# An adaLN attention and mixture-of-experts block in fp32: a reordered seam before the first expert, split products in the prologue, and a reordered expert loop

## What is computed

```
mod = silu(c) @ wmod -> sa, ca, ga, sb, cb, gb        (4 x 512 each; ga, gb kept off zero)
h = layernorm(x) * (1 + ca) + sa
x = x + ga * attention(h)       16 segments of 128 tokens per batch: softmax(Q K^T * scale) V in each,
                                plus attention among the segments' first tokens, times Wo, biases
h = layernorm(x) * (1 + cb) + sb                       8192 tokens x 512
score = softmax(h @ Wg + bg)    16 experts; gate = max, idx = argmax
pos = rank of the token within its expert; keep = pos < 512
y = relu(h @ W1[idx] + b1[idx]) @ W2[idx] + b2[idx]    W1 512 x 2048, W2 2048 x 512 for each expert
x = x + gb * where(keep, y * gate, 0)
```

## Time and profile before

| | before |
|---|---|
| median of 3 runs | 1816.24 us (1816.03 to 1816.32) |
| the profiled execution | 1814.79 us |
| its span | 1813.2 us |
| PE busy | 1779.8 us (98%) |
| DVE busy | 1112.3 us (61%) |
| ACT busy | 893.4 us (49%) |
| POOL busy | 610.1 us (34%) |
| mean granted clock of TensorE | 0.995 of full |

### The profile page before, as it was taken

One profiled execution on the slowest core, in us unless ns is written; L12 is line 12 of the kernel. 1 busy time (PEld: TensorE's weight loads), 2 busy tenths in 40 slices (PEclk: granted clock), 3 DMA queues, 4 the chain that ended last, 5 costly groups with the idle time before them and its releaser, 6 DMA issues.

```text
span 1813.2 us, 27903 instructions
## 1 busy us (share of the span) xinstructions
PE 1779.8 (98%) x9135; PEld 1489.6 (82%) x9136; DVE 1112.3 (61%) x1964; ACT 893.4 (49%) x1317; POOL 610.1 (34%) x565
## 2 busy tenths in 40 slices
PE   9999999999999799999999999998998999999998
PEld 5788888888888488898888888888888888888886
DVE  6577887887887644445445444457558675444753
ACT  4446546546546344354444444347467664434741
POOL 1145555555554511123030303043225431304303
PEclk9999999999999899999999999999999999999999
DMA  7586767777777454344453524265446553426522
GB/s 278 183 228 186 197 157 204 180 173 200 188 193 221 95 174 160 112 168 167 144 169 107 174 98 162 98 207 197 158 141 225 197 212 129 155 98 211 201 80 79
DMA packets 148429, 304.09 MB, mean 168 GB/s; under 512 B 18097, under 2 KB 18493, under 8 KB 146326
## 3 DMA queue, kind: packets, MB, share of 16 engines
q1 hardware_dynamic: 115098, 221.01, 35.0%
q0 software_dynamic: 33280, 82.42, 18.8%
HBM read 254.29 MB, written 67.43 MB: 177 GB/s over the span
## 4 chain that ended last, share of the span: by engine, by line
PE 89%; DVE 1%; ACT 1%; issue 1%; DMA 1%; POOL 0%; POOLq 0%; ACTq 0%; DVEq 0%
PE bank L344 27%; PE bank L346 27%; PE bank L345 27%; PE bank L778 3%; PE bank L962 1%; PE bank L875 1%; PE bank L649 1%; PE bank L770 1%; DMA h_rows<-xr 1%; ACT h_f L1304 0%; PE bank L753 0%; ACT h_hi L1303 0%; PE bank L748 0%; DVE w_lo L1746 0%; PE bank L785 0%
## 5 line engine op out<-in xcount | busy, mean ns | idle before, releaser
L1303 ACT ACTIVATE h_hi<-bank,b_col 128x512 fp32r<-128x512 f32 x256 | 176.8, 691 | 526.1 <-PE bank L346 474.9
L1773 DVE TENSOR_TENSOR h_lo<-h_f,h_hi 128x512 fp32r<-128x512 f32 x256 | 174.0, 691 | 349.9 <-ACT h_f L1304 270.7
L344 PE MATMUL bank<-bt_hi,w_hi 128*128 128x512 f32 (+4 forms) x1024 | 359.1, 351 | 3.9 <-DVE w_lo L1746 3.5
L345 PE MATMUL bank<-bt_lo,w_hi 128*128 128x512 f32 (+4 forms) x1024 | 358.0, 350 | 0.0
L346 PE MATMUL bank<-bt_hi,w_lo 128*128 128x512 f32 (+4 forms) x1024 | 358.0, 350 | 0.0
L344 PE MATMUL bank<-w_hi,h_hi 128*128 128x512 f32 x832 | 325.8, 392 | 1.0 <-issue 1.0
L345 PE MATMUL bank<-w_lo,h_hi 128*128 128x512 f32 x832 | 324.2, 390 | 0.0
L346 PE MATMUL bank<-w_hi,h_lo 128*128 128x512 f32 x832 | 323.9, 389 | 0.0
L2069 POOL DMA_INDIRECT out_dram<-yo,tok_x x64 | 75.4, 1178 | 671.7 <-DVE yo L1808 636.4
L344 PEld LDWEIGHTS bank<-bt_hi,w_hi 128*128 128x128 f32 x1024 | 193.2, 189 | 28.8 <-issue 5.6
L345 PEld LDWEIGHTS bank<-bt_lo,w_hi 128*128 128x128 f32 x1024 | 193.3, 189 | 21.2 <-issue 0.2
(11 more groups left out here) (312 smaller groups left out, 2938.0 us busy)
## 6 DMA issues: line engine op xcount, KB each, us to landing
raw<-in_L_ffn_W_dram SPq DMA_DIRECT2D x128, 1024.0 KB
xa<-in_L_attn_x_dram SPq DMA_DIRECT2D x16, 1024.0 KB, 8.5
xr<-in_L_attn_x_dram SPq DMA_DIRECT2D x16, 1024.0 KB, 6.8
xr<-global_rows POOLq DMA_DIRECT2D x16, 1024.0 KB, 8.6
h_rows<-sb_tab SPq DMA_DIRECT2D x16, 1024.0 KB
out_dram<-xr SPq DMA_DIRECT2D x16, 1024.0 KB, 10.7
h_rows<-h POOLq DMA_DIRECT2D x15, 1024.0 KB
b_bc<-in_L_ffn_b_dram SPq DMA_DIRECT2D x16, 256.0 KB, 6.3
```

The source lines that it names most:

```text
L344: pe.matmul(o, a_hi, b_hi, start=start, stop=False)
L345: pe.matmul(o, a_hi, b_lo, start=False, stop=False)
L1303: act.activation(h1_hi[b % 2][:, j, :], h_bank[j][:, :], ACT.Relu, bias=bias)
L1773: dve.tensor_tensor(h1_lo[b % 2][:, j, :], h1_f[:, j, :], h1_hi[b % 2][:, j, :].bitcast(F32), ALU.subtract) \
```

## The change

**Prologue.** The product of Wq and Wk, 16 fp32 matmuls, becomes three float32r products, with eight casts on ACT and eight subtractions on DVE ahead of them. **Last turns.** The four scalings of Z's rows go from DVE (`scale_rows`) to POOL, which stores the rows in two halves; POOL's scatter of Z2 goes from ahead of the store to behind the first expert's gather. The finder of the first expert's rows covers Z2, Z1 and Z (Z1 and Z before), and `first_index` is one operation, ahead of the writing of Z's `slot_i`. **First block.** The first expert's first block runs in two halves of 256 columns, the rows 256 to 511 first; the second block's W1 is rounded ahead of the first block's ReLU. **Expert loop.** The transposes for the next expert go into the middle of tile 0 of `results(e, 2)`; DVE makes the next expert's `bt_lo` ahead of `w2_low` of block 3, runs `gate_results` in block 0 and `add_results` earlier in block 2.

```diff
...
+        sp.wait_ge(scattered[Z3.par], 16 * GS * (Z3.half + 1))
+        sp.wait_ge(scattered[Z2.par], 16 * GS * Z2.half)
         sp.wait_ge(u_full, 4 * NG)
         slots = table_dram.rearrange("(e p j) c -> p e j c", p=P, j=GS)
         sp.dma_start(first_tab[:], slots[:, 0, :, :]).then_inc(first_in, 16)
+        iteration(Group(NG // 2, 0), False, True, False)
...
-        for _ in range(6):
+        for _ in range(8):
             pe.matmul(banks[7][:, 0:P], ident[:], ident[:], start=True, stop=True)
         for k in range(KC):
-            pe.wait_ge(wqk_in[k], 32)
+            pe.wait_ge(pro_hi_done, 2 * k + 2)
             for c in range(KC):
-                last = pe.matmul(pro_bank(MCH + c)[:, :], wq_s[:, k, chunk(c)], wk_s[:, k, :],
-                                 start=(k == 0), stop=(k == KC - 1))
+                pe.matmul(pro_bank(MCH + c)[:, :], wq_hi[:, k, chunk(c)], wk_hi[:, k, :], start=(k == 0), stop=False)
+            pe.wait_ge(split_made, 2 * k + 2)
+            for c in range(KC):
+                pe.matmul(pro_bank(MCH + c)[:, :], wq_hi[:, k, chunk(c)], wk_lo[:, k, :], start=False, stop=False)
+                last = pe.matmul(pro_bank(MCH + c)[:, :], wq_lo[:, k, chunk(c)], wk_hi[:, k, :], start=False,
+                                 stop=(k == KC - 1))
...
-            ranks(Z1)
-            quarters(Z)
+            quarters(Z, lambda: ranks(Z1))
             pe.wait_ge(parts_out, Z.n + 1)
             pe.wait_ge(lg_step, Z1.n + 1)
             turn_parts()
             first_slots(0)
+            first_slots(1)
             ranks(Z)
-            first_slots(1)
+            first_slots(2)
...
+                    if between is not None and j == 0 and c == HC // 2:
+                        between()
...
+        def first_half(cols, j):
+            for k in range(KC):
+                if cols is LATE and j == 0:
+                    pe.wait_ge(first_low, 2 + k + 1)
+                elif j == 0:
+                    pe.wait_ge(bt_split, k + 1)
+                last = split3(pe, h_bank[j][:, cols], w1_hi[0][:, k, chunk(j)], w1_lo[0][:, k, chunk(j)],
+                              bt_hi[:, k, cols], bt_lo[:, k, cols], k == 0, k == KC - 1)
+            if cols is EARLY:
+                last.then_inc(h1_full, 1)
+        def first_block():
+            first_tile(3)
+            keep_busy(1, h_bank[1])
+            first_tile(2)
+            keep_busy(1, h_bank[1])
+            first_half(LATE, 0)
+            first_tile(1)
+            first_half(LATE, 1)
+            first_tile(0)
+            pe.wait_ge(first_low, 2 + KC + 1)
+            first_half(LATE, 2)
+            pe.wait_ge(w1_split, 1)
+            first_half(LATE, 3)
+            for j in range(HC):
+                first_half(EARLY, j)
...
-        keep_busy(3, y_bank[0])
-        gathered_transpose(0, None)
+        keep_busy(3, h_bank[1])
         first_expert()
...
+            act.wait_ge(wqk_in[k], 32)
+            act.activation(wk_hi[:, k, :], wk_s[:, k, :], ACT.Copy).then_inc(pro_hi_done, 1)
+            act.activation(wq_hi[:, k, :], wq_s[:, k, :], ACT.Copy).then_inc(pro_hi_done, 1)
...
+            dve.tensor_tensor(wk_lo[:, k, :], wk_s[:, k, :], wk_hi[:, k, :].bitcast(F32), ALU.subtract) \
+                .then_inc(split_made, 1)
+            dve.wait_ge(pro_hi_done, 2 * k + 2)
+            dve.tensor_tensor(wq_lo[:, k, :], wq_s[:, k, :], wq_hi[:, k, :].bitcast(F32), ALU.subtract) \
...
         def first_index():
-            dve.wait_ge(first_in, 16)
-            dve.tensor_copy(first_f[:, 0, :], first_tab[:, :, 0]).then_inc(first_step, 1)
-            row, segment = t1_last[:, 0:GS], t1_last[:, GS:2 * GS]
-            shift, whole, total = first_f[:, 1, :], first_f[:, 2, :], first_f[:, 3, :]
             dve.wait_ge(first_full, 1)
-            dve.tensor_scalar(shift, row, 0.0, float(Z1.n * ROWS - 1 - NO_TOKEN), ALU.is_gt, ALU.mult) \
-                .then_inc(first_step, 1)
             dve.wait_ge(first_step, FIRST_TAB)
-            dve.scalar_tensor_tensor(out=whole, in0=segment, scalar=float(P), in1=first_f[:, 0, :], op0=ALU.mult,
-                                     op1=ALU.add).then_inc(first_step, 1)
-            dve.wait_ge(first_step, FIRST_TAB + 2)
-            dve.tensor_tensor(total, row, whole, ALU.add).then_inc(first_step, 1)
-            dve.wait_ge(first_step, FIRST_TAB + 3)
-            dve.tensor_tensor(tok_h[:], shift, total, ALU.add).then_inc(tok_h_ready, 1)
+            dve.tensor_tensor(tok_h[:], t1_last[:, 0:GS], first_f[:, 0, :], ALU.add).then_inc(tok_h_ready, 1)
...
+            if which == 2:
+                first_index()
             dve.wait_ge(route, r + 14)
             wait_past(dve, scattered[g.par], 16 * GS * g.half)
...
-            route_slots(Z2)
-            dve.wait_ge(x2_stored[Z1.par], 16 * (Z1.half + 1))
+            route_slots(Z2, 0)
             route_logits(Z1)
-            for s in range(GS):
-                scale_rows(s)
-            route_slots(Z1, 0)
+            route_slots(Z1, 1)
             route_logits(Z)
-            route_slots(Z, 1)
+            route_slots(Z, 2)
...
+                if b == 2 and not first:
+                    add_results(e - 1)
                 for j in range(1, HC):
                     split_hidden(e, b, j)
+                if b == NB - 1 and not last:
+                    rows_low(e + 1)
                 w2_low(n, b)
                 if b == 0 and first:
...
                     next_index(e)
                 if b == 0 and not first:
                     result_rows(e - 1)
-                if b == 1 and not first:
                     gate_results(e - 1)
...
                 if b == 2:
                     if not first:
-                        add_results(e - 1)
...
-            scatter(Z2)
-            store_h2(Z, xr[Z1.par])
-            for par in range(2):
-                pool.wait_ge(h2_stored[par], 16 * (NG // 2))
+            scaled = xr[Z1.par]
+            pool.wait_ge(x2_stored[Z1.par], 16 * (Z1.half + 1))
+            pool.wait_ge(shift_stored[Z.par], 16 * (Z.half + 1))
+            for lo in (0, 2):
+                for s in (lo, lo + 1):
+                    pool.wait_ge(xn2_done, 4 * Z.n + s + 1)
+                    pool.tensor_tensor(scaled[:, s, :], h2[Z.par][:, s, :], cb_tab[:, batch_of(Z), :], ALU.mult) \
+                        .then_inc(h2_ready, 1)
+                pool.wait_ge(h2_ready, 4 * Z.n + lo + 2)
+                pool.dma_start(group_rows(h2_dram, Z)[:, lo:lo + 2, :], scaled[:, lo:lo + 2, :], accum_op=ALU.add) \
+                    .then_inc(h2_stored[Z.par], 16)
+            pool.wait_ge(h2_stored[Z1.par], 16 * (Z1.half + 1))
+            pool.wait_ge(h2_stored[Z.par], 16 * (Z.half + 2))
             pool.wait_ge(xh_cleared, GS)
             gather_h(0)
+            pool.wait_ge(first_in, 16)
+            scatter(Z2)
             scatter(Z1)
             scatter(Z)
...
```

More of the change, by code:

```diff
@@ L196, in build_block @@
     wv_hi, wv_lo = over(r_split, ("wv_hi", full, F32R), ("wv_lo", full, F32R))
+    wk_hi, wk_lo = over(r_v, ("wk_hi", full, F32R), ("wk_lo", full, F32R))
+    wq_hi, wq_lo = over(r_m, ("wq_hi", full, F32R), ("wq_lo", full, F32R))
     wo_hi, = over(r_gt, ("wo_hi", full, F32R))
@@ L826, in first_slots @@
                 for s in range(GS):
-                    last = pe.matmul(t1_last[:, 0:2 * GS], first_sel[:, which, s, :],
-                                     first_pick[:, which, s, :, :].rearrange("p a j -> p (a j)"), start=(which == 0 and s == 0),
-                                     stop=(which == 1 and s == GS - 1))
-                if which == 1:
+                    for part in range(2):
+                        last = pe.matmul(t1_last[:, 0:GS], first_sel[:, which, s, :], first_pick[:, which, s, part, :],
+                                         start=(which == 0 and s == 0 and part == 0),
+                                         stop=(which == 2 and s == GS - 1 and part == 1))
+                if which == 2:
                     last.then_inc(first_full, 1)
@@ L939, in rows_of, with filled_tiles @@
             return pe.value_load(expert_rows[0:1, bass.ds(e, 1)], min_val=0, max_val=T)
-        def filled_tiles(rows, tile, passed_over=lambda: None, between=lambda: None):
+        def filled_tiles(rows, tile, passed_over=lambda: None):
             for j in range(GS - 1, 0, -1):
@@ L951, in filled_tiles @@
                     passed_over()
-            between()
             tile(0)
@@ L964, in tile @@
                         last.then_inc(bt_full, 1)
-                if rows is None:
-                    keep_busy(2 if j == 0 else 1, y_bank[0])
             filled_tiles(rows, tile)
@@ L998, in hidden, with results @@
             narrowest(range(256, ROWS + 1, 64))
-        def results(e, b, rows, between=lambda: None):
+        def results(e, b, rows, between=None):
             n = NB * e + b
@@ L1309, in rows_high @@
```

(14 more changed lines are left out.)

93 lines of the change are left out of this document (62 added, 31 removed).

## The result

The changed kernel takes 1836.26 us (median of 5 runs, 1836.02 to 1838.36) where the kernel before takes 1816.32 (5 runs beside it): 1.1% slower, ratio 1.0113, 95% interval 1.0100 to 1.0127. The prediction was slower, 1820.7, with a range to 1825.5: the side was right, the size was a quarter of what came, and the range missed it.

The account below looks back on a forecast made before the run. PE, busy in 98% of the span, was taken to bound the kernel. Prologue 0, seam +11.3 and expert loop −6.8 summed to +4.5, so 1816.24 became 1820.7 us, with a range of 1812.5 to 1825.5.

Parts of the forecast that it names:

- What bounds the kernel: Whole kernel: PE works in 98% of the span, so reordering can win back only 33 us of idle PE.
- Prologue, 0: Start: PE is ready up to 3.6 us sooner but waits for the unmoved load of `wm_b`; gain 0.
- Seam, +11.3: Before the first expert: Z's `slot_i` and PE wait for Z2's scatter behind the gather; 11.3 us lost, bounds 8.1 and 13.3.
- the upper bound of 5.2: Last turns: POOL's four scalings hold up DVE's small routing steps by between 0 and 5.2 us; 3.2 taken.
- the sum was 33.6: Seam: time from the gather's start at 614.0 to the end of the first expert's first block at 647.6.
- Expert loop, −6.8: Experts: shorter waits gain 3.5 in expert 7 and 4.3 in expert 9, less 1.0 for late lo parts; bounds −3.5 and −9.9.
- The ReLU comes 1.75 earlier with its block.: Expert 7: without the 1.75 wait for W1, the last ReLU before the transposes comes 1.75 earlier.
- The late `bt_lo`, taken as 1.0: Expert hand-overs: later transposes may make first products of experts with few columns wait for lo parts; 1.0 over the run.
- The 7.8 of the two experts: Experts 7 and 9: predicted gains of 3.5 and 4.3 from shorter waits for W1 and the ReLU.
- The rival: Expert hand-overs: each of 15 waits some 0.6 for `bt_lo`, +9.0 instead of +1.0, total 1828.7; chance 0.05.
- The seam's own rivals: Seam: scalings don't hold DVE up, 1817.5, chance 0.16; or the seam works as arranged, 1805.8, chance 0.12.
- late lo parts: Expert loop rival: later transposes make 15 hand-overs wait some 0.6 each for `bt_lo`, +9.0, total 1828.7; chance 0.05.

Follow-up runs that it names:

- the fastest: Z2's scatter and loop order restored, scalings on DVE, then `gate_results` in block 0, ReLUs before next W1, `rows_low` before `w2_low` except first expert: 1805.33 us, ratio 0.9937.

## Why the prediction missed

By the trace, 21.5 more: start −0.9, seam +13.1 (the first product 11.9 later beyond the start's gain, the first expert 1.2 longer), the rest of the loop +9.2. I had 0, +11.3 and −6.8.

- **What bounds the kernel: right, but read too narrowly.** PE's second longest wait was not the one for W1 (3.5) but one for DVE's `onehot` in the last turns (L737, 3.6), which became 6.4 (L749) with POOL's scalings beside DVE, and 2.8 with them back on DVE. I read three stretches that the change touches. The largest new loss in the loop fell in expert 1, which I didn't look at.
- **Prologue, 0: right in kind.** `wm_b` is what PE waits for once the product is shorter: all ten experiments show such a wait, 0.5 to 2.4 long, the longest of them here; where the load lands early, as in the changed kernel's profile, 0.9 remains. The start itself scatters: with the same prologue the groups' turns began 1.1 earlier to 1.6 later than before. The latest is the execution with the longest wait, in which the clock then stood at half for 3.4.

```profile
21.67 0.59 PE L609 MATMUL bank<-wk_s,bias_col 128*1 128x512 f32 x1 [2.36 <-DMA wm_b<-in_L_wmod_dram]
```

- **Seam, +11.3: right, measured 13.1.** The wait, its place and its chain were as worked out. The step that was too small is DVE's hold-up. Three small steps took 1.27, 1.21 and 3.45 where without POOL's scalings they take 0.17, 0.23 and 0.15: 5.4 lost, the upper bound of 5.2 and not the 3.2 that I took. The last of them ended at 602.57, 0.02 behind the whole second pair of POOL's scalings (599.62 to 602.55), so no step slipped in between there; beside the first pair one did (0.15 at 597.20), as I had assumed. By the Trainium skill (SBUF — State Buffer, section "SBUF: two separate sides") whichever of a DVE step with two SBUF inputs and a GpSimd instruction that reads SBUF starts first has the shared ports for its whole instruction, and the other blocks. The trace agrees that DVE's step ended with POOL's work, but it was held for two instructions, though it is shown as starting at 599.12, 0.50 ahead of the first of them. The hand-over from `tok_h` to the gather took 1.08 and not 0.6. From the gather on, the sum was 33.6 and came to 32.4 (616.14 to 648.57).
- **Expert loop, −6.8: wrong in sign, and the whole miss.** The loop cost 9.2, 16.0 more than I had. Three steps failed, worth 6.8, 3.1 and 6.1 of it (the last with all that expert 1 lost).
  1. "The ReLU comes 1.75 earlier with its block." It doesn't: the ReLUs stand on ACT behind the next expert's W1, whose load landed 39.5 after the expert's first product in the changed kernel (1266.7 less 1227.2). Before, ACT came to that rounding 39.0 after the first product (1206.25) and went straight on; in expert 9 it had to wait 0.12 there, until 39.2. So the load came hardly earlier then, and PE's own lateness hid it: I saw no idle time on ACT. The 7.8 of the two experts were 1.0.
  2. The late `bt_lo`, taken as 1.0, cost 4.1. It hit wide experts too, by 0.3 to 0.4 each, and went with the transposes back ahead of tile 0. The rival had it at 9.0.
  3. Putting `rows_low` ahead of `w2_low` was costed at nothing. But `rows_low` waits for the transposes, so `w2_low`, and SP's loads into the buffer that it frees, waited with it, for some 11 us (6.2 ahead of the next first product, then 4.6 behind it). In the one place where PE had a stall of its own, the loop's first pass, the loads met it: +5.2 with the clock, most of the 6.1 that expert 1 lost. That is a queue behind a moved wait, which I had looked for on DVE at the seam and not here.
- **The rivals.** The seam's own rivals fell; "late lo parts" was half true. No case of mine held a cost in expert 1, so nothing reached 1836.

## What to carry to other kernels

Where a wait is moved ahead of an operation that frees a buffer, follow the buffer: the load that waits for it is late by as much, and it shows up where nothing was moved. When a wait is taken away, ask which load lands next, also if no idle time shows it yet: an engine's lateness can hide a load exactly. And two losses that look like one, a count behind a gather and a late load, are told apart by undoing each alone and then both: here the single gains add up to the whole (12.3 + 7.7 = 20.0 of 19.9), and with both undone nothing is left of it.

## What the runs showed of the hardware

The stall in expert 1 is in all twelve traces, 0.95 to 3.31 long. In each, one 16 KB packet of the instruction queue begins just ahead of it or in it, and a second one 3.0 to 4.0 later, about when the product starts. The first began 1.72 ahead of PE's last product in the kernel before (stall 0.99), 0.36 ahead with Z2's scatter moved (2.79), 0.19 ahead with the transposes moved (2.89), and 0.23 after it in the changed kernel (3.31); in the eight kernels where the first expert's `rows_low` is late as before, 1.65 to 2.62 ahead, with stalls of 0.95 to 1.48. In ten of the twelve the product came 3.07 to 3.28 after that packet's start (2.70 in the kernel before, 3.80 in the fastest). So the stall is about 3 less that lead, and not much under 1: PE seems to wait for code that it runs for the first time, and the packet is late where the DMA engines are busy. They were at 0.92 in the stretch up to the end of the stall in the changed kernel and at 0.34 before:

```profile
721.00:729.00 8.00, 4.69 (x25) 4.01 (x23) 4.29 (x5) 6.30 (x8) 5.78 (x4) 0.95 0.92 320
```

```profile
709.00:714.30 5.30, 4.31 (x23) 3.66 (x21) 3.59 (x3) 3.64 (x7) 0.52 (x1) 1.00 0.34 97
```

The packet is late in the three kernels in which the loads are late, and in none of the other nine. That it is PE's code in that packet is inferred from time and place and not shown, nor is how the loads delay it.
